# Attention phases in another order, GpSimd splitting the negated maxima, row transfers moved in SP's queue

## What is computed

```
scores = einsum('bhqd,bhkd->bhqk', q, k) * HD ** -0.5
scores = where(causal, scores, -inf)
w = softmax(scores, axis=-1)
a = einsum('bhqk,bhkd->bhqd', w, v)
out = a.transpose(0, 2, 1, 3).reshape(B, S, D) @ Wo + bo
```

## Time and profile before

| | us |
|---|---|
| median of 3 runs | 949.21 |
| span of the profiled execution | 947.1 |
| first attention stage, `at0`, from its first product | 77.2 to 215.5 |
| second attention stage, `at1` | 348.3 to 487.1 |

### The profile page before, as it was taken

The page is one execution under the profiler, slowest core; times in us unless marked ns, Lnnn a source line. Parts: engine busy times, 40 slices in busy tenths (PEclk is TensorE's granted clock), DMA queues, the critical chain, the costliest instruction groups (busy, mean ns, idle before and its releaser), DMA issues. The chain is left out here.

```text
span 947.1 us, 12745 instructions
## 1 busy us (share of the span) xinstructions
PE 819.3 (87%) x4477; PEld 508.3 (54%) x4477; DVE 620.1 (65%) x1318; ACT 390.9 (41%) x665; POOL 149.4 (16%) x205
## 2 busy tenths in 40 slices
PE   5556899997899897999997997778999999779896
PEld 3253343325688563344345796445556666447675
DVE  6887888826775688788636787453167671266774
ACT  3241456682621343566775433441122222133553
POOL 1500121130020001112310000104112221100143
PEclk9866899999999987899999998999999999989998
DMA  6326300000000454200006100894201110220000
GB/s 198 105 85 194 122 8 2 2 2 1 1 1 1 148 179 157 68 2 3 1 1 128 2 1 1 287 381 150 75 23 45 51 44 30 63 93 1 1 23 24
DMA packets 49557, 64.00 MB, mean 68 GB/s; under 512 B 12534, under 2 KB 34806, under 8 KB 49494
## 3 DMA queue, kind: packets, MB, share of 16 engines
q1 hardware_dynamic: 47302, 57.52, 19.7%
q0 software_dynamic: 1872, 5.13, 1.5%
q10 hardware_dynamic: 320, 0.52, 0.2%
HBM read 50.30 MB, written 15.51 MB: 69 GB/s over the span
## 5 line engine op out<-in xcount | busy, mean ns | idle before, releaser
L855 DVE TENSOR_REDUCE at1mx<-at1ps_s 128x1 f32<-128x512 f32 (+3 forms) x152 | 90.6, 656 | 19.9 <-PE at1ps_s L757 11.1
L855 DVE TENSOR_REDUCE at0mx<-at0ps_s 128x1 f32<-128x512 f32 (+3 forms) x152 | 90.7, 656 | 19.0 <-PE at0ps_s L757 11.1
L835 ACT ACTIVATE at1probs<-at1ps_e 128x1024 f32<-128x1024 f32 (+3 forms) x96 | 73.8, 809 | 47.9 <-PE at1ps_e L778 47.6
L835 ACT ACTIVATE at0probs<-at0ps_e 128x1024 f32<-128x1024 f32 (+3 forms) x96 | 73.8, 809 | 47.0 <-PE at0ps_e L778 46.7
L1137 PE MATMUL f2ps<-gu_raw,f2xT_b 128*128 x184 | 82.9, 593 | 1.0 <-ACT f2xT_b L1224 1.0
L1242 ACT ACTIVATE f2sg<-f2ps 128x512 f32<-128x512 f32 x30 | 17.8, 597 | 130.4 <-PE f2ps L1137 100.9
L754 PE MATMUL at0ps_s<-ks,qs 96*128 96x512 bf16 (+3 forms) x192 | 58.0, 364 | 5.1 <-DMA ks<-scratch 3.6
L754 PE MATMUL at1ps_s<-ks,qs 96*128 96x512 bf16 (+3 forms) x192 | 58.0, 361 | 2.5 <-DMA ks<-scratch 1.0
L1321 DVE TENSOR_TENSOR f2h<-f2sg,f2ps 128x512 f32<-128x512 f32 x30 | 20.5, 686 | 60.5 <-ACT f2sg L1242 29.0
L1137 PEld LDWEIGHTS f2ps<-gu_raw,f2xT_b 128*128 128x128 f32 x184 | 34.8, 190 | 35.5 <-issue 34.4
L778 PE MATMUL at1ps_e<-qs,ks 99*128 99x512 bf16 (+3 forms) x192 | 46.9, 341 | 5.3 <-DMA qs<-at1rows 3.4
(11 more groups left out here) (434 smaller groups left out, 1783.5 us busy)
## 6 DMA issues: line engine op xcount, KB each, us to landing
gu_raw<-in_L_ffn_w_gate_up SPq DMA_DIRECT2D x8, 1024.0 KB, 13.2
scratch<-parts SPq DMA_DIRECT2D x8, 768.0 KB, 3.9
qs<-scratch SPq DMA_DIRECT2D x48, 128.0 KB, 2.6
ks<-scratch SPq DMA_DIRECT2D x44, 128.0 KB, 2.7
dn_raw<-in_L_ffn_w_down SPq DMA_DIRECT2D x8, 512.0 KB, 12.3
f2x_in<-slots_in SPq DMA_DIRECT2D x23, 129.0 KB, 2.0
slots_in<-in_c_empty SPq DMA_DIRECT2D x1, 2944.0 KB, 18.8
traw<-in_L_ffn_w_gate_up SPq DMA_DIRECT2D x1, 2048.0 KB, 10.0
```

The lines of the kernel that those rows point to most:

```text
L835: act.activation(probs[:, slots(v), 0:n], ps_e[:, v % SCORE_PAIRS, :, 0:n], ACT.Exp, scale=HD ** -0.5)\
L855: dve.tensor_reduce(mx[:, p % 2, lo // CH, j:j + heads, t], rows_of, AX.X, ALU.max).then_inc(s_red, 1)
```

## The change

It has four parts. `PHASES` becomes (0,0), (1,0), (2,0), (0,1), (1,1), (2,1), (3,1), (3,0): the short first halves of three groups, then the second halves, and the first half of group 3 at the end. The split of the maxima moves from VectorE to GpSimd, where a list `PICKS` places it among the selects; VectorE negates in the reduction, and only merges two minima where a phase is a second half. In SP's queue, pieces 2 and 3 are written at the end of `split_stage` instead of behind group 1's reads. The three weight loads `a1` move from `n2` to the second attention stage, behind group 3's reads.

```diff
@@ split_stage, SP
             read_stack(sp, m, 0, 1, range(BY_SP))
+            write(2)
+            write(3)
-PHASES = [(g, qc) for g in range(GROUPS) for qc in range(NC)]
+PHASES = [(0, 0), (1, 0), (2, 0), (0, 1), (1, 1), (2, 1), (3, 1), (3, 0)]
+NEEDS = [max(g for g, _ in PHASES[:p + 1]) for p in range(len(PHASES))]
+SECOND = [p for p, (_, qc) in enumerate(PHASES) if qc == 1]
@@ order_of_products
-    signal, place, split, late = 0.1, 3.2, 1.15, 1.0e9
+    signal, place, split, merge, late = 0.1, 3.2, 1.3, 0.25, 1.0e9
...
                 if n + 1 == MAXIMA_UP_TO[p]:
-                    vector += split
-                    split_at[p] = vector + signal
+                    if p in SECOND:
+                        vector += merge
+                    picks.append((vector + signal, ("split", p)))
+                    pool = max(pool, vector + signal) + split
+                    split_at[p] = pool + signal
@@ attention_stage, TensorE
-                if qc == 0 and (n == 0 or MAXIMA[n - 1][0] < p):
-                    pe.wait_ge(m.stacked, (g + 1) * STACK_SIGNALS)
+                if n == 0 or NEEDS[MAXIMA[n - 1][0]] < NEEDS[p]:
+                    pe.wait_ge(m.stacked, (NEEDS[p] + 1) * STACK_SIGNALS)
@@ attention_stage, GpSimd
+            def split_max(p):
+                high, middle, low = (mst[:, p % 2, :, k, :] for k in range(MP))
+                if p in SECOND:
+                    pool.wait_ge(m_least, SECOND.index(p) + 1)
+                    least = nm[:, SECOND.index(p) % 2]
+                else:
+                    pool.wait_ge(s_red, MAXIMA_UP_TO[p])
+                    least = mx[:, p % 2, 0]
+                if p >= 2:
+                    pool.wait_ge(m_turned, p - 1)
+                c.step(pool.tensor_copy(high, least))
+                c.step(pool.tensor_tensor(rest[:], least, high, ALU.subtract))
+                c.step(pool.tensor_copy(middle, rest[:]))
+                pool.tensor_tensor(low, rest[:], middle, ALU.subtract).then_inc(m_split, 1)
+
+            for kind, n in PICKS:
+                if kind == "select":
+                    select(n)
+                else:
+                    split_max(n)
@@ attention_stage, VectorE
+                if p >= 2 and (n == 0 or MAXIMA[n - 1][0] < p):
+                    dve.wait_ge(m_split, p - 1)
-                dve.tensor_reduce(mx[:, p % 2, lo // CH, j:j + heads, t], rows_of, AX.X, ALU.max).then_inc(s_red, 1)
+                dve.tensor_reduce(mx[:, p % 2, lo // CH, j:j + heads, t], rows_of, AX.X, ALU.max, negate=True).then_inc(s_red, 1)
+            def merge(p):
                 dve.wait_ge(s_red, MAXIMA_UP_TO[p])
-                if p >= 2:
-                    dve.wait_ge(m_turned, p - 1)
-                high, middle, low = (mst[:, p % 2, :, k, :] for k in range(MP))
-                if PHASES[p][1] == 0:
-                    c.step(dve.tensor_scalar(nm[:], mx[:, p % 2, 0], -1.0, None, ALU.mult))
-                else:
-                    c.step(dve.tensor_tensor(nm[:], mx[:, p % 2, 0], mx[:, p % 2, 1], ALU.max))
-                    c.step(dve.tensor_scalar(nm[:], nm[:], -1.0, None, ALU.mult))
-                c.step(dve.tensor_copy(high, nm[:]))
-                c.step(dve.tensor_tensor(rest[:], nm[:], high, ALU.subtract))
-                c.step(dve.tensor_copy(middle, rest[:]))
-                dve.tensor_tensor(low, rest[:], middle, ALU.subtract).then_inc(m_split, 1)
+                dve.tensor_tensor(nm[:, SECOND.index(p) % 2], mx[:, p % 2, 0], mx[:, p % 2, 1], ALU.min).then_inc(m_least, 1)
@@ attention_stage, SP
             read_group(1)
-            for n in range(2, 4):
-                write_parts(sp, m, n)
             place(0)
             for n in range(2, 4):
                 sp.wait_ge(m.written[n], 16)
             read_group(2)
             place(1)
             read_group(3)
+            for dst, src, s in loads:
+                sp.dma_start(dst, src).then_inc(s, 16)
             for p in range(2, len(PHASES)):
                 place(p)
@@ build
-                loads += on("a1", ffn_loads(raw0, "L1G", "L1U", "L1D"))
-                attention_stage(nc, ctx, m, "at1", v_all, oT, l1b[:, 3 * D:4 * D])
+                attention_stage(nc, ctx, m, "at1", v_all, oT, l1b[:, 3 * D:4 * D],
+                                loads=on("a1", ffn_loads(raw0, "L1G", "L1U", "L1D")))
```

More of the change, by code:

```diff
@@ L615, in order_of_products @@
     pair = item = step = done = 0
-    rows, order = [], []
+    rows, order, picks = [], [], []
     def advance():
@@ L629, in advance @@
                 if p > 0 and s == FIRST_STEP[p] + 1 and done % (GH // PAIR) == 1 and p - 1 not in copied:
+                    if FIRST_STEP[p] - 1 not in summed:
+                        return
                     scalar = copied[p - 1] = max(scalar, summed[FIRST_STEP[p] - 1]) + 0.6
@@ L633, in advance @@
                 if queries_of(s)[2]:
+                    picks.append((scalar + signal, ("select", done)))
                     pool = max(pool, scalar + signal) + 0.41
@@ L688, in order_of_products @@
             item += 1
-    return order
-ORDER = order_of_products()
+    return order, [pick for _, pick in sorted(picks)]
+ORDER, PICKS = order_of_products()
 MAXIMA_BY = [sum(kind == "max" for kind, _ in ITEMS[:i + 1]) for i in range(len(ITEMS))]
@@ L697, in attention_stage @@
 @stage
-def attention_stage(nc, ctx, m, tag, v_all, oT, out_bias):
+def attention_stage(nc, ctx, m, tag, v_all, oT, out_bias, loads=()):
     qs, ks = m.stacks
     s_full, s_red = sem(nc, ctx, tag + "_s_full"), sem(nc, ctx, tag + "_s_red")
-    m_split, m_turned, m_out = (sem(nc, ctx, tag + x) for x in ("_m_split", "_m_turned", "_m_out"))
+    m_least, m_split, m_turned, m_out = (sem(nc, ctx, tag + x) for x in ("_m_least", "_m_split", "_m_turned", "_m_out"))
     placed = [sem(nc, ctx, tag + "_placed%d" % i) for i in range(2)]
@@ L720, in attention_stage @@
         mx = sb("mx", [P, 2, NC, GH, TILES])
-        nm, rest = (sb(n, [P, GH, TILES]) for n in ("nm", "rest"))
+        nm = sb("nm", [P, 2, GH, TILES])
+        rest = sb("rest", [P, GH, TILES])
         mst = sb("mst", [P, 2, GH, MP, TILES], BF16)
@@ L840, in _, with select @@
         def _(pool):
-            for n, v in enumerate(DIAGONAL):
+            c = Chain(pool, chain)
+            def select(v):
                 pool.wait_ge(exp_done, v + 1)
@@ L845, in _ @@
                     .then_inc(masked, 1)
+            def split_max(p):
[17 more added lines that the diff above has]
+                    split_max(n)
         @block.vector
         def _(dve):
-            c = Chain(dve, chain)
             def maximum(i, n):
@@ L853, in maximum @@
                 dve.wait_ge(s_full, n + 1)
+                if p >= 2 and (n == 0 or MAXIMA[n - 1][0] < p):
+                    dve.wait_ge(m_split, p - 1)
                 rows_of = ps_s[:, i % MAX_BANKS, 0:heads * width].rearrange("p (h n) -> p h n", h=heads)
-                dve.tensor_reduce(mx[:, p % 2, lo // CH, j:j + heads, t], rows_of, AX.X, ALU.max).then_inc(s_red, 1)
-            def split_max(p):
+                dve.tensor_reduce(mx[:, p % 2, lo // CH, j:j + heads, t], rows_of, AX.X, ALU.max, negate=True).then_inc(s_red, 1)
+            def merge(p):
                 dve.wait_ge(s_red, MAXIMA_UP_TO[p])
-                if p >= 2:
-                    dve.wait_ge(m_turned, p - 1)
-                high, middle, low = (mst[:, p % 2, :, k, :] for k in range(MP))
-                if PHASES[p][1] == 0:
-                    c.step(dve.tensor_scalar(nm[:], mx[:, p % 2, 0], -1.0, None, ALU.mult))
-                else:
-                    c.step(dve.tensor_tensor(nm[:], mx[:, p % 2, 0], mx[:, p % 2, 1], ALU.max))
-                    c.step(dve.tensor_scalar(nm[:], nm[:], -1.0, None, ALU.mult))
-                c.step(dve.tensor_copy(high, nm[:]))
-                c.step(dve.tensor_tensor(rest[:], nm[:], high, ALU.subtract))
-                c.step(dve.tensor_copy(middle, rest[:]))
-                dve.tensor_tensor(low, rest[:], middle, ALU.subtract).then_inc(m_split, 1)
+                dve.tensor_tensor(nm[:, SECOND.index(p) % 2], mx[:, p % 2, 0], mx[:, p % 2, 1], ALU.min).then_inc(m_least, 1)
             for i, (kind, n) in enumerate(ITEMS):
@@ L874, in _ @@
                     maximum(i, n)
-                    if n + 1 == MAXIMA_UP_TO[MAXIMA[n][0]]:
-                        split_max(MAXIMA[n][0])
+                    if MAXIMA[n][0] in SECOND and n + 1 == MAXIMA_UP_TO[MAXIMA[n][0]]:
+                        merge(MAXIMA[n][0])
             dve.tensor_tensor(m.x[:], m.x[:], out_bias.unsqueeze(1).to_broadcast([P, T, D]), ALU.add)
```

## The result

| | before | after |
|---|---|---|
| median of the runs, us | 949.82 (948.98 to 953.17, 4 runs) | 981.23 (976.46 to 982.84, 4 runs) |
| span of the profiled execution, us | 947.1 | 980.1 |
| mean granted clock of TensorE | 0.942 | 0.924 |

The ratio is 1.0313, with an interval of 1.0278 to 1.0348. Slower was right; 959 and the range of 949 to 968 were not. The loss lies in the two attention stages: 151.3 us against 138.2 in the first, 159.0 against 138.8 in the second, 33.3 together; the span grew by 33.0.

A forecast was written before the change was run, and what follows sets the result against it. TensorE was taken to bound the middle of each attention stage, VectorE 7 us behind. Two stages of 3.8 - 0.9 = 2.9 us plus 3.5 for the loads gave +9.3 on 949.2: 958.5, rounded to 959, range 949 to 968.

The forecast's parts named there:

- the tail: End of each attention stage: the same exponentials set the pace after the last two phases change places; cost 0.
- the port: Stage end: the last GpSimd split waits out VectorE's addition to x; 2.3 us a stage, 963 us in all; chance 0.10.
- Group 2: Opening of a stage: TensorE out of work near 95, standing some 7 us until group 2's reads land at 102.0.
- Group 1: Opening of a stage: group 1's reads land at 87.0, and the first score pair starts 1.8 us later than before.
- The term for the two writes: Scratch writes issued ahead of group 1's reads delay those reads by 0 to 1.05 us; 0.5 taken.
- The work behind: After phase 1's last score pair TensorE is behind by 3.0 us of maxima and scores and 0.2 of values.
- the clock: TensorE's lower clock after the stand for group 2: 2 us added, between 0 and 5.
- VectorE's relief: Split moved to GpSimd: VectorE saves 8.3 us a stage, buying at most TensorE's 0.95 us idle in the middle; 0.9 taken.
- The loads: Second stage: three weight loads stand before row transfer 2 and delay phase 2's scores; 3.5 us taken, from 1 to 7.4.
- the rival's 7.4: Second stage: row transfer 2's rows land after the last weight load, costing 7.4 us; with another clock fall 964; chance 0.11.
- the four rivals: VectorE sets the middle (943.7, 0.15); about 4 us a stage return (949.8, 0.12); split waits (963, 0.10); loads wait (964, 0.11).
- the forecast's own signs of being wrong: Group 2 landing before TensorE asks, the middle shrinking by more than 3 us, or reductions with negation taking longer.

The follow-up runs named there:

- e3: The changed kernel with the old order of phases, everything else as changed: 948.45 us, 0.9978 of the kernel before.
- e7: e3 with VectorE's addition to x moved to the start of each attention stage: 941.53 us, 0.9893 of the kernel before.
- e8: e3 with the last two phases swapped, so the short half of the fourth group comes last: 947.40 us, 0.9948 of the kernel before.
- e4: The kernel before with only the maxima negated by the reduction and split on GpSimd: 952.67 us, 1.0025 of the kernel before.
- e13: The kernel before with only the addition to x moved to the start of the attention stage: 952.34 us, 1.0017 of the kernel before.
- e17: e4 with the addition to x moved to the start of the stage: 941.27 us, 0.9905 of the kernel before.
- e6: The changed kernel with the addition to x moved to the start of each attention stage: 975.85 us, 1.0246 of the kernel before.
- e1: The changed kernel with the three weight loads back in the second normalization: 972.69 us, 1.0219 of the kernel before.
- e15: The changed kernel with loads back in the normalization, addition to x first, reads of groups 1 and 2 half on each queue: 955.18 us, 1.0045 of before.

## Why the prediction failed, step by step

The step that failed is the end of the sum: it followed TensorE to the last pair of phase 1 and counted no wait behind that (the tail at 0, the port only as a rival at 0.10). The rows of phase 3, which the order had only put off, and the last split each made TensorE stand there, and the lower clock followed both times. Besides, group 1's reads and the loads were priced too low. In the first stage's 13.1 us, against 2.9 forecast, the opening is 3.2 (0.6), the work behind it 2.8 (3.2), the clock behind it 3.4 (0) and idle time behind it 3.7 (-0.9).

**Group 2 (right).** TensorE stood 7.58 us against 7 forecast, ended by these reads, with VectorE and ScalarE idle. Both ends came over 3 us later than forecast (98.0 and 105.6, against 95 and 102.0), 1.8 of it with the first product.

**Group 1 (too small).** The forecast had it land at 87.0, 9.8 us behind the first product; it landed 11.1 us behind it (79.00 to 90.09), and TensorE stood 5.10 us. The term for the two writes, 0.5, was too small: behind them the first six reads took 4.89 us to issue and landed 3.4 us after their issue, against 3.75 and 2.6 in before. In e3, e7 and e8, which have the writes there too, it is 4.0 to 4.5 and 3.1 to 3.5 us; in e4, e13 and e17, which don't, 3.75 and 2.6 to 2.7. DMA issues of after from 78.5 to 90:

```profile
qs<-scratch SPq DMA_DIRECT2D x6, 128.0 KB, 3.4
ks<-scratch SPq DMA_DIRECT2D x6, 128.0 KB, 3.1
```

The first score pair starts at 96.47, 17.5 us behind the first product (79.00) against 14.1 in the earlier trace rows: 3.4 us later instead of 1.8. The opening to the sixteenth pair is 47.0 us instead of 43.84: +3.2, forecast +0.6. (The forecast calls that pair in before, which ends at 121.04, the last of phase 1; it is the sixteenth there, and its sum uses it as such.)

**The work behind (right), the clock (too small).** From there to the end TensorE has 97.39 us of work instead of 91.17. 6.8 us of this stretch run at the lower clock (141.0 to 144.4 and the same length from 209.2), which costs half of that, 3.4; what is left, 2.8, is the forecast's 3.2. The forecast had priced one fall of the clock with 2 us; there were two more, each behind a short stand: at the rows of phase 3 and at the last split.

```profile
141.00:144.40 3.40, 3.40 (x14) 1.77 (x15) 1.13 (x3) 1.86 (x2) 0.00 (x0) 0.50 0.00 0
209.20:212.60 3.40, 3.40 (x18) 0.33 (x10) 0.00 (x0) 2.28 (x3) 0.00 (x0) 0.50 0.02 4
```

**VectorE's relief (right, and hidden here).** The forecast took 0.9 us of idle time away from the middle; idle time behind phase 1 rose from 3.19 to 6.91 us, by the waits of the next two paragraphs. VectorE's busy time fell by 6.1 us a stage, not by 8.3. In the old order, with the addition moved, the relief can be seen: from e13 to e17 (negation and split on GpSimd) the stages shorten from 137.9 and 137.7 to 135.9 and 135.6, 2 us each. The 68.70 us of the first stage that the earlier trace rows shows from 121.3, counted from each run's first product, first in e13 and then in e17:

```profile
125.10:193.80 68.70, 67.75 (x524) 27.88 (x523) 60.38 (x118) 44.27 (x64) 14.86 (x37) 1.00 0.01 2
```

```profile
124.40:193.10 68.70, 68.65 (x529) 27.49 (x527) 56.05 (x97) 45.41 (x66) 19.00 (x57) 1.00 0.01 2
```

TensorE's work there rises from 67.75 to 68.65 us. So the middle gave back 0.9 us, as the bound said. The other 1.1 us lie in the opening and at the end (0.7 and 0.2 us of idle time) and in the busy time; the term left these out.

**The rows of phase 3 (missing).** Three short phases have 24 exponential pairs, and 27 wide maxima of phase 3 must be reduced before its rows can be turned. The gap of 7.6 us between the exponentials isn't new. The old order has it from phase 0 to phase 1 (e3: 7.7 us, with 2.0 us of TensorE's idle time), and in before TensorE is idle 2.1 us there and the clock falls behind it:

```profile
103.35:110.60 7.25, 5.19 (x50) 2.28 (x49) 7.04 (x17) 0.66 (x2) 0.41 (x1) 1.00 0.01 2
110.60:114.00 3.40, 3.40 (x11) 1.32 (x12) 1.50 (x3) 2.05 (x2) 0.00 (x0) 0.53 0.59 187
```

In after it is 2.7 us (126 to 141). So at the sixteenth pair the kernel before has this gap behind it and the changed one still ahead. The forecast compared the two there, followed the order no further and counted only work from there on.

**The tail (wrong).** It was put at 0, and the port rival at 0.10, because TensorE "still has scores ahead of that turn". They ran out: TensorE waited 1.86 us and then had the lower clock. The rival's mechanism is the one measured: 2.25 us for a cast beside the addition, forecast price 2.3 a stage; e6 gave 5.4 for both. The Trainium skill (SBUF — State Buffer, section Who interferes with whom) has the rule that a VectorE instruction with two SBUF inputs shuts out a GpSimd instruction that reads SBUF for its whole length; e4's select (2.49 us) and the casts of after (2.25) and e8 (2.19) agree, and e6's cast (0.20) shows the other side.

**The loads (too small).** 3.5 was taken, the rival's 7.4 was right, and a little low: 8.19 us, 8.5 by e1. In after the first issue of row transfer 2 came at 406.3. The last load, issued at 405.8, landed 10.2 us later, at 416.0, and TensorE went on at 416.33, so the rows landed about as late as all three loads; SP's timeline and the DMA issue:

```profile
405.76 0.47 SPq L924 DMA_DIRECT2D raw_dn<-in_L1D  x1
406.27 5.63 SPq L914 DMA_DIRECT2D qs<-at1rows  x4
...
raw_dn<-in_L1D SPq DMA_DIRECT2D x1, 1024.0 KB, 10.2
```

The parts of the forecast, 2 x 2.9 + 3.5 = 9.3, were 2 x 13.1 + 7.1: the sign was found, but two of the four rivals, which the sum leaves out, came true at once, and the order wasn't followed to its end. The landmarks say the same: the idle stretch at group 2 was there, but a second one of over 5 us stood ahead of it at group 1, and the last maximum came at 203.4 instead of 193. None of the forecast's own signs of being wrong came; they all looked at terms that it had.

## What to carry to other kernels

When the order of work changes, ask for every operand of the new order when it lands, at the rate of the whole queue ahead of it, and follow the new order to the first place where it is as far as the old one in waits as well as in work, not to the first landmark. A short stand of TensorE has to be priced with the low clock behind it: here 1.7 us each, behind stands of 2.3 us in all (rows of phase 3) and 1.9 us (last split). Before small dependent steps move to GpSimd, look for a long VectorE instruction with two inputs beside them; with the addition to x moved to the start (e17), the same split that lost 0.25% alone wins 0.95%.

## What the runs showed that was not expected

- A negating reduction costs the same: 684 ns over 96 reductions of 512 elements, before and after.

```profile
L855 DVE TENSOR_REDUCE at0mx<-at0ps_s 128x1 f32<-128x512 f32 x96 | 61.2, 684 | 9.9 <-PE at0ps_s L754 7.3 <-PE at0ps_s L757 2.1
```

```profile
L889 DVE TENSOR_REDUCE at0mx<-at0ps_s 128x1 f32<-128x512 f32 x96 | 61.0, 684 | 9.2 <-PE at0ps_s L765 4.6 <-PE at0ps_s L768 4.1 <-issue 0.3
```

- The busy share of the DMA engines isn't their rate: reads of 128 KB on two queues keep them busy all the time at 210 GB/s (e15), the same reads on one queue 0.66 of the time at 202 GB/s, while 1 MB loads reach 335 GB/s in a window with a share of 0.89.
- The small split steps take 0.20 to 0.22 us on GpSimd at a distance of 0.28, so a whole split takes 1.06 us, as on VectorE.
